# Clamps on GpSimd as a minimum and then a maximum in one instruction, and a semaphore for each down product, in a fused recurrent block

## The chip, the cores and the metric

The kernel runs on one core of a Trainium2 chip. The metric is the device time of one execution in microseconds. The kernel before took 123.34 us (median of three runs, 123.24 to 123.43). The profile is of one execution of its own; in it the first and the last recorded instruction are 121.0 us apart.

Engines: PE is TensorE (PEld its weight loads), DVE is VectorE, ACT is ScalarE, POOL is GpSimd, SP is the engine that issues most DMAs. Each engine takes its instructions strictly in the order in which the program lists them, and waits between engines are semaphores that are counted up.

## The reference

The input x has the shape (8, 512, 128): eight sequences of 512 steps with 128 channels, in float32. Cut to what matters:

```
xn   = layernorm(x)
kin, vin, rin = xn * m + shifted(xn) * (1 - m)        # one m for each of the three
k, v, r = kin @ Wk, vin @ Wv, sigmoid(rin @ Wr)
mx_t  = max(mx_{t-1} + td, k_t)                       # running maximum
den_t = exp(mx + td - mx_t) * den + exp(k - mx_t)     # and the same for the numerator
s    = (r * numerator / denominator) @ Wo
f    = relu(xn @ W1 + b1) @ W2 + b2                   # 128 -> 512 -> 128
g    = silu(layernorm(xn + f) * gamma + beta)
out  = x + s * g
```

## The kernel before

The work is tiled by sequence: b = 0 to 7, each with tiles of 128 channels (partitions) by 512 steps. For each b some fifty steps are named, and the strings in PROGRAM give, engine by engine, the order in which each engine does them; the steps of two or three sequences are interleaved, and most tiles have two buffers, so that b waits for b - 2. BANKS gives each of the eight PSUM banks the list of the results that it holds one after the other; `bank_free` makes a result wait for the last reader of the result before it in its bank (FREED_BY).

The steps that matter here, with the lines of the profile:

- POOL: `norm1:b` (L335, xn, four instructions of 128x128), `d:b` (L365, step_x), `xT_hi:b` and `xT_lo:b` (L349, L356: the transposed input in two fp32r parts), `fix:b` (L374), `gmin:b` (`lower`, L382), `gmax:b` (`upper`, L389), `dv:b` (L396), `keep:b` (L404), `nm` (L326, for groups of sequences).
- `gap:b` (DVE, L729) is k minus the running maximum before it. `gmin:b` is min(gap, td) and `gmax:b` is max(gap, td), td being a column of one value for each partition. ACT makes exp of each: `e_new:b` (L496, from gap_min) and `e_keep:b` (L512, from gap_max).
- DVE then scans `den:b` (L736), ACT takes its logarithm (`ln_den`, L500), DVE makes `rel` (L744), ACT `th_g` and `th_a` (L525, L504), POOL `keep`, DVE scans `dev` (L751), then `adev`, `wkv`, `gated` (L759, L767, L775).
- PE: `T:b` transposes xn (L566), `up0` to `up3` (L601 to L603, three matmuls each in fp32r), `k`, `v`, `r` (L581), `z0` to `z3` (L632, the four down products that add up in one bank), `var` (L618), `s` (L611), `back` (L643). An fp32 product of 512 columns stands in the profile as two matmuls.
- ACT `hid0` to `hid3` (L468) are the relu, `sq` (L477) the square of z + b2, `ln_var`, `rstd2`; DVE `zn` (L784), ACT `silu` (L536), DVE `prod` (L792) and `res` (L801).

The order of POOL between the first clamp and the third sequence is `xT_lo:1 gmax:0 nm:2 gmin:0 norm1:2 gmin:1 gmax:1 dv:0 d:2 xT_hi:2 xT_lo:2`, and later `d:4 fix:4 gmin:3 gmax:3 xT_lo:4 norm1:5`.

Of the four down products of a sequence only the last in PE's order counts a semaphore up, `done["z"]`; `sq:b` waits for it, and `hid` of b waits for that of b - 2.

## Time and profile before

| | |
|---|---|
| median of three runs | 123.34 us |
| lowest, highest | 123.24, 123.43 us |
| the profiled execution | 122.89 us |
| its span, first to last instruction | 121.0 us |
| PE busy | 105.6 us (87%) |
| DVE busy | 96.4 us (80%) |
| ACT busy | 95.0 us (79%) |
| POOL busy | 79.8 us (66%) |
| mean granted TensorE clock | 0.972 of full speed |

The span is shorter than the time by 1.9 us, which lie around it. Busy time counts an instruction from its start to its end. On PE, and to a lesser degree on the others, an instruction starts before the one ahead of it has ended, so that the distance from start to start is shorter than a duration: the pace of two instructions is read from their starts.

### The profile page before, as it was taken

What the parts mean: (1) busy time and instruction counts of PE and PEld (TensorE: products, weight loads), DVE (VectorE), ACT (ScalarE), POOL (GpSimd) and SP (SyncE); (2) the same over time, 40 slices, a digit from 0 to 9 for tenths busy, and PEclk for the clock granted to TensorE, in tenths of its full rate; (3) what the DMA queues carried; (4) which work ended last, traced back from release to release, by engine and by line L of the source; (5) the groups of instructions that cost most, each with busy time, mean ns of one, the idle gap of its engine ahead of it and who ended that gap; (6) DMA issues with size and microseconds to landing.
All of it is one profiled execution on the core that took longest, in us unless ns stands there. A gap on an engine that the chain in (4) does not pass through costs nothing. (4 is left out here: it accounts for less than half of the span.)

```text
span 121.0 us, 1604 instructions
## 1 busy us (share of the span) xinstructions
PE 105.6 (87%) x336; PEld 56.7 (47%) x336; DVE 96.4 (80%) x199; ACT 95.0 (79%) x155; POOL 79.8 (66%) x104
## 2 busy tenths in 40 slices
PE   5996997864999989997599999999979789999770
PEld 5961353613455535642456464465433435544340
DVE  1769897369969599998746789995999396989991
ACT  2361759298969979995769999996999599999960
POOL 2069999986356899269999988946746980380000
PEclk9999999997699999999859999999999999999999
DMA  4999000000000000000000230000000002022035
GB/s 112 270 312 250 12 3 0 5 0 0 0 3 3 0 0 0 0 0 0 0 0 0 87 93 1 0 0 0 0 3 0 3 0 86 1 87 87 5 105 155
DMA packets 9449, 5.09 MB, mean 42 GB/s; under 512 B 480, under 2 KB 9184, under 8 KB 9440
## 3 DMA queue, kind: packets, MB, share of 16 engines
q1 hardware_dynamic: 8880, 4.59, 13.4%
q10 hardware_dynamic: 560, 0.40, 1.3%
q8 instruction: 3, 0.05, 0.2%
q14 instruction: 6, 0.05, 0.1%
HBM read 2.89 MB, written 2.10 MB: 41 GB/s over the span
## 5 line engine op out<-in xcount | busy, mean ns | idle before, releaser
L632 PE MATMUL bank<-hid,w_c 128*128 128x512 f32 x64 | 31.4, 594 | 0.0
L581 PE MATMUL bank<-mixed,w_in 128*128 128x512 f32 x48 | 25.4, 624 | 1.7 <-DVE prod L792 0.6
L468 ACT ACTIVATE hid<-bank,vec 128x512 f32<-128x512 f32 x32 | 21.4, 681 | 2.3 <-PE bank L603 1.9
L601 PE MATMUL bank<-xT_hi,w_hi 128*128 128x512 f32 x28 | 16.5, 588 | 5.3 <-POOL xT_lo L356 5.3
L712 DVE SCALAR_TENSOR_TENSOR mixed<-step_x,vec,bank 128x511 f32<-128x511 f32 x24 | 17.5, 736 | 1.1 <-POOL step_x L365 1.1
L632 PEld LDWEIGHTS bank<-hid,w_c 128*128 128x128 f32 x64 | 12.2, 194 | 10.9 <-issue 9.7
L736 DVE TENSOR_TENSOR_SCAN den<-e_keep,bank 128x512 f32<-128x512 f32 x8 | 9.7, 1216 | 8.2 <-ACT e_keep L512 3.9
L389 POOL TENSOR_SCALAR gap_max<-gap,td 128x512 f32<-128x512 f32 x8 | 12.5, 1561 | 3.8 <-DVE gap L729 3.8
L581 PEld LDWEIGHTS bank<-mixed,w_in 128*128 128x128 f32 x48 | 8.4, 194 | 11.9 <-issue 8.8
L382 POOL TENSOR_SCALAR gap_min<-gap,td 128x512 f32<-128x512 f32 x8 | 12.5, 1561 | 1.9 <-DVE gap L729 1.9
L365 POOL TENSOR_TENSOR step_x<-xT 128x512 f32<-128x512 f32 x8 | 9.0, 1127 | 6.4 <-ACT xT L460 6.3
L396 POOL TENSOR_TENSOR dv<-v_sb 128x512 f32<-128x512 f32 x8 | 9.6, 1205 | 4.8 <-ACT v_sb L519 4.8
L601 PEld LDWEIGHTS bank<-xT_hi,w_hi 128*128 128x128 f32 x28 | 5.5, 197 | 14.8 <-issue 9.5
L335 POOL TENSOR_SCALAR xn<-x_sb,neg_mean,rstd 128x128 f32<-128x128 f32 x28 | 12.1, 446 | 0.0
L751 DVE TENSOR_TENSOR_SCAN dev<-keep,dv 128x512 f32<-128x512 f32 x8 | 9.8, 1224 | 2.3 <-POOL dv L396 1.5
L602 PE MATMUL bank<-xT_hi,w_lo 128*128 128x512 f32 x28 | 11.6, 413 | 0.0
L603 PE MATMUL bank<-xT_lo,w_hi 128*128 128x512 f32 x28 | 11.5, 411 | 0.0
L721 DVE TENSOR_TENSOR_SCAN mx<-td,bank 128x512 f32<-128x512 f32 x8 | 9.7, 1210 | 0.8 <-PE bank L581 0.6
L418 ACT ACT_TABLE_LOAD x6 | 7.7, 1283 | 2.3 <-issue 2.2
L611 PE MATMUL bank<-gated,wo_half 128*128 128x512 f32 (+1 forms) x18 | 8.5, 553 | 0.9 <-DVE gated L775 0.9
L618 PE MATMUL bank<-sq,averager 128*128 128x512 f32 (+1 forms) x18 | 9.1, 601 | 0.1
L512 ACT ACTIVATE e_keep<-gap_max,td 128x512 f32<-128x512 f32 x8 | 5.8, 720 | 4.2 <-POOL gap_max L389 4.2
(70 smaller groups left out, 204.1 us busy)
## 6 DMA issues: line engine op xcount, KB each, us to landing
x_sb<-x SPq DMA_DIRECT2D x7, 256.0 KB, 6.3
block_out<-res SPq DMA_DIRECT2D x7, 256.0 KB, 2.3
w_in<-squares SPq DMA_DIRECT2D x1, 256.0 KB, 3.1
w_in<-w ACTq DMA_DIRECT2D x1, 256.0 KB, 5.6
w_in<-w SPq DMA_DIRECT2D x1, 256.0 KB, 5.9
block_out<-res SPq DMA_DIRECT2D x2, 128.0 KB, 1.9
x_sb<-x ACTq DMA_DIRECT2D x1, 128.0 KB, 2.5
x_sb<-x SPq DMA_DIRECT2D x1, 128.0 KB, 2.2
```

What stands on the lines that cost most here:

```text
L335: pool.tensor_scalar(xn[n][:, j, :], x_tile(b, j), neg_mean1[:, i:i + 1], rstd1[:, i:i + 1], ALU.add, ALU.mult).then_inc(done["norm1"], 1)
L382: pool.tensor_scalar(gap_min[n][:, :], gap[n][:, :], td[:, :], None, ALU.min).then_inc(done["gmin"], 1)
L389: pool.tensor_scalar(gap_max[n][:, :], gap[n][:, :], td[:, :], None, ALU.max).then_inc(done["gmax"], 1)
L468: act.activation(hid[b % 2][:, f, :], ps(f"up{f}", b)[:, :], ACT.Relu, bias=vec[:, B1_COLUMN + f:B1_COLUMN + f + 1]).then_inc(done[f"hid{f ...
L581: pe.matmul(ps(name, b)[:, :], w_in[:, which, :], mixed[b % 2][:, which, :], start=True, stop=True).then_inc(done[name], 1)
L601: pe.matmul(dst, hi, xT_hi[n][:, :], start=True, stop=False)
L602: pe.matmul(dst, lo, xT_hi[n][:, :], start=False, stop=False)
L603: pe.matmul(dst, hi, xT_lo[n][:, :], start=False, stop=True).then_inc(done[f"up{f}"], 1)
L632: ins = pe.matmul(ps("z", b)[:, :], w2_c[:, f, :], hid[b % 2][:, f, :], start=False, stop=last, skip_group_check=True)
L712: dve.scalar_tensor_tensor(mixed[n][:, which, 1:], step_x[n][:, 1:], vec[:, which:which + 1], ps("z", b)[:, 0:T - 1], ALU.mult, ALU.add).t ...
L721: dve.tensor_tensor_scan(mx[n][:, 1:], td[:, 0:1].to_broadcast([P, T]), ps("k", b)[:, :], MX_START, ALU.add, ALU.max).then_inc(done["mx"], 1)
L751: dve.tensor_tensor_scan(dev[n][:, :], keep[n][:, 0:T], dv[n][:, :], 0.0, ALU.mult, ALU.add).then_inc(done["dev"], 1)
```

## The change

Two things are edited and the schedule strings are changed with them. First, `lower` and `upper` get a second operation each: min(gap, td) is followed by a maximum with the most negative float32, and max(gap, td) is preceded by a minimum with the largest float32, so that both are one instruction with a minimum and then a maximum; the values are what they were. Second, each down product counts up a semaphore of its own, `hid{f}:b` waits for product f of b - 2 alone, and `sq:b` waits for the last of the four in PE's order. On PE `z3:0` moves ahead of `z2:0`, and `up1:7` ahead of `z0:6`; on DVE `zn:5` ahead of `inr:7`; on POOL `nm:4` ahead of `xT_hi:3`. Several results move to another PSUM bank. ACT's order and the DMAs stay.

```diff
--- before.py
+++ after.py
...
 MX_START = -1e38
+FP32_MAX = 3.4028234e38
 WARM_UP = 11
...
     "pe": """
-        T:0 up3:0 b2m up2:0 k:0 T:1 up0:0 up1:0 v:0 k:1 up1:1 up0:1 up2:1 z0:0 z1:0 T:2 up3:1 z2:0 z0:1
-        z1:1 z3:0 up3:2 r:0 z3:1 z2:1 k:2 var:0 up2:2 up0:2 v:1 up1:2 z2:2 T:3 z0:2 var:1 s:0 z1:2 r:1
+        T:0 up3:0 b2m up2:0 k:0 T:1 up0:0 up1:0 v:0 k:1 up1:1 up0:1 up2:1 z0:0 z1:0 T:2 up3:1 z3:0 z2:0
+        z0:1 z1:1 up3:2 r:0 z3:1 z2:1 k:2 var:0 up2:2 up0:2 v:1 up1:2 z2:2 T:3 z0:2 var:1 s:0 z1:2 r:1
         v:2 z3:2 up3:3 up2:3 up0:3 r:2 T:4 k:3 up1:3 z0:3 z2:3 var:2 z1:3 k:4 z3:3 up3:4 up0:4 var:3
...
         up2:5 var:4 up1:6 up2:6 up0:5 v:5 T:7 k:6 z0:5 s:3 z2:5 up0:6 z1:5 z3:5 r:5 up3:6 z2:6 k:7 var:5
-        z1:6 up3:7 z0:6 up1:7 z3:6 up0:7 back:2 var:6 v:6 s:4 up2:7 back:3 v:7 z0:7 back:4 z1:7 z2:7 r:6
+        z1:6 up3:7 up1:7 z0:6 z3:6 up0:7 back:2 var:6 v:6 s:4 up2:7 back:3 v:7 z0:7 back:4 z1:7 z2:7 r:6
         r:7 z3:7 s:5 var.a:7 var.b:7 back:5 s:6 s.a:7 back:6 s.b:7 back.a:7 back.b:7
...
         dev:3 adev:3 wkv:3 dev:4 adev:4 wkv:4 gated:3 prod:2 gated:4 mx:5 gap:5 inr:5 ink:6 inv:6 zn:4
-        den:5 mx:6 rel:5 inr:6 prod:3 ink:7 dev:5 adev:5 gap:6 wkv:5 gated:5 mx:7 gap:7 den:6 inr:7 zn:5
+        den:5 mx:6 rel:5 inr:6 prod:3 ink:7 dev:5 adev:5 gap:6 wkv:5 gated:5 mx:7 gap:7 den:6 zn:5 inr:7
         inv:7 res:2 den:7 prod:4 rel:6 zn:6 res:3 rel:7 dev:6 adev:6 res:4 wkv:6 dev:7 gated:6 prod:5
...
         d:0 w1_lo nm:1 fix:0 norm1:1 w2_c d:1 xT_hi:1 fix:1 xT_lo:1 gmax:0 nm:2 gmin:0 norm1:2 gmin:1
-        gmax:1 dv:0 d:2 xT_hi:2 xT_lo:2 keep:0 fix:2 norm1:3 keep:1 gmax:2 gmin:2 dv:1 d:3 xT_hi:3 nm:4
+        gmax:1 dv:0 d:2 xT_hi:2 xT_lo:2 keep:0 fix:2 norm1:3 keep:1 gmax:2 gmin:2 dv:1 d:3 nm:4 xT_hi:3
         fix:3 xT_lo:3 norm1:4 dv:2 keep:2 xT_hi:4 d:4 fix:4 gmin:3 gmax:3 xT_lo:4 norm1:5 norm1:6 gmax:4
...
 z:0 s:0 up0:3 up1:3 k:4 k:5 k:7 s:6 back:6
-up3:0 up0:0 v:0 up2:2 up1:2 var:1 r:1 z:4 s:3 r:5 up3:7 up0:7 s:4 v:7
-b2m z:1 up2:3 k:3 s:2 up1:6 up0:6 up3:6 var:5 up1:7 var:6 up2:7 r:6 var.a:7
-up2:0 k:1 v:2 var:3 z:5 back:2 back:3 back:4 var.b:7
-k:0 var:0 v:1 up3:3 r:2 up0:4 up2:4 up1:5 z:6
+up3:0 up0:0 v:0 up2:2 up1:2 var:1 r:1 k:3 s:2 up1:6 up0:6 up3:6 var:5 up1:7 back:2 back:3 back:4 var.b:7
+b2m z:1 up3:3 r:2 up0:4 up2:4 up3:5 r:4 up2:6 z:7
+up2:0 k:1 v:2 var:3 z:5 up0:7 s:4 v:7
+k:0 var:0 v:1 up2:3 z:4 s:3 r:5 up3:7 var:6 up2:7 r:6 var.a:7
 up1:0 up1:1 r:0 up0:2 z:3 v:4 up2:5 v:5 v:6 s:5 back:5 s.b:7 back.b:7
-up0:1 up3:1 up3:2 k:2 var:2 up3:4 up1:4 back:0 back:1 up3:5 r:4 up2:6 z:7
+up0:1 up3:1 up3:2 k:2 var:2 up3:4 up1:4 back:0 back:1 up1:5 z:6
 up2:1 z:2 s:1 v:3 r:3 var:4 up0:5 k:6 r:7 s.a:7 back.a:7
...
                  + [f"up{f}" for f in range(NF)] + [f"hid{f}" for f in range(NF)]
-                 + ["z", "sq", "var", "ln_var", "rstd2", "zn", "silu", "prod", "back", "res"])
+                 + [f"z{f}" for f in range(NF)] + ["sq", "var", "ln_var", "rstd2", "zn", "silu", "prod", "back", "res"])
         done = {n: sem(f"done_{n}") for n in STEPS}
...
                     after(eng, step, previous[2], previous[1])
+
+        def chunks_of(b):
+
+            return [name for name, _, i in tokens("pe") if name in CHUNKS and i == b]
...
                 after(pool, "e_new", b - 2)
-                pool.tensor_scalar(gap_min[n][:, :], gap[n][:, :], td[:, :], None, ALU.min).then_inc(done["gmin"], 1)
+                pool.tensor_scalar(gap_min[n][:, :], gap[n][:, :], td[:, :], -FP32_MAX,
+                                   ALU.min, ALU.max).then_inc(done["gmin"], 1)
...
                 after(pool, "e_keep", b - 2)
-                pool.tensor_scalar(gap_max[n][:, :], gap[n][:, :], td[:, :], None, ALU.max).then_inc(done["gmax"], 1)
+                pool.tensor_scalar(gap_max[n][:, :], gap[n][:, :], FP32_MAX, td[:, :],
+                                   ALU.min, ALU.max).then_inc(done["gmax"], 1)
...
                     after(act, f"up{f}", b)
-                    after(act, "z", b - 2)
+                    after(act, f"z{f}", b - 2)
                     act.activation(hid[b % 2][:, f, :], ps(f"up{f}", b)[:, :], ACT.Relu,
...
                 once(act, b, "cols", 4)
-                after(act, "z", b)
+                after(act, chunks_of(b)[-1], b)
                 after(act, "var", b - 2)
...
                 pe.wait_ge(got["vec"], 16)
+                bank_free(pe, "b2m", None)
                 pe.wait_ge(prep["consts"], 2)
...
                     once(pe, b, "w2", 1)
-                    order = [name for name, _, i in tokens("pe") if name in CHUNKS and i == b]
-                    if order[0] == f"z{f}":
+                    if chunks_of(b)[0] == f"z{f}":
...
                     after(pe, f"hid{f}", b)
-                    last = order[-1] == f"z{f}"
-                    ins = pe.matmul(ps("z", b)[:, :], w2_c[:, f, :], hid[b % 2][:, f, :], start=False, stop=last,
-                                    skip_group_check=True)
-                    if last:
-                        ins.then_inc(done["z"], 1)
+                    pe.matmul(ps("z", b)[:, :], w2_c[:, f, :], hid[b % 2][:, f, :], start=False,
+                              stop=chunks_of(b)[-1] == f"z{f}", skip_group_check=True).then_inc(done[f"z{f}"], 1)
                 return step
...
```

## Rows read from the trace of the kernel before

**Rows 1.** page: busy us, share of the span and count, by engine

```profile
PE 105.6 (87%) x336; PEld 56.7 (47%) x336; DVE 96.4 (80%) x199; ACT 95.0 (79%) x155; POOL 79.8 (66%) x104
```

**Rows 2.** POOL by line and form; behind the bar busy us, mean ns

```profile
L389 POOL TENSOR_SCALAR gap_max<-gap,td 128x512 f32<-128x512 f32 x8 | 12.5, 1561 | 3.8 <-DVE gap L729 3.8
L382 POOL TENSOR_SCALAR gap_min<-gap,td 128x512 f32<-128x512 f32 x8 | 12.5, 1561 | 1.9 <-DVE gap L729 1.9
L335 POOL TENSOR_SCALAR xn<-x_sb,neg_mean,rstd 128x128 f32<-128x128 f32 x28 | 12.1, 446 | 0.0
...
L404 POOL TENSOR_SCALAR keep<-th_g 128x512 f32<-128x512 f32 x8 | 5.0, 620 | 3.5 <-ACT th_g L525 3.5
...
L374 POOL TENSOR_SCALAR mixed<-vec,step_x 128x3 f32<-128x3 f32 x8 | 2.6, 331 | 3.4 <-PE bank L581 3.2
...
L326 POOL TENSOR_SCALAR neg_mean<-mv 128x16 f32<-128x16 f32 x1 | 0.3, 266 | 0.0
...
L326 POOL TENSOR_SCALAR neg_mean<-mv 128x4 f32<-128x4 f32 x1 | 0.2, 239 | 0.0
```

**Rows 3.** timeline of POOL: start us, duration us, line, operation [idle before]

```profile
16.32 1.56 POOL L389 TENSOR_SCALAR gap_max<-gap,td 128x512 f32<-128x512 f32 x1
...
22.87 1.56 POOL L389 TENSOR_SCALAR gap_max<-gap,td 128x512 f32<-128x512 f32 x1
```

**Rows 4.** timeline of ACT, the exponentials behind the first clamps and the last

```profile
22.93 0.69 ACT L496 ACTIVATE bank<-gap_min,neg_td 128x512 f32<-128x512 f32 x1 [1.89 <-POOL gap_min L382]
24.47 0.72 ACT L512 ACTIVATE e_keep<-gap_max,td 128x512 f32<-128x512 f32 x1 [0.85 <-POOL gap_max L389]
...
96.21 0.69 ACT L496 ACTIVATE bank<-gap_min,neg_td 128x512 f32<-128x512 f32 x1 [1.47 <-POOL gap_min L382]
```

**Rows 5.** timeline of PE: start us, duration us, line [idle before <-releaser]

```profile
28.84 0.76 PE L601 MATMUL bank<-xT_hi,w_hi 128*128 128x512 f32 x1 [2.57 <-POOL xT_lo L356]
...
46.11 0.71 PE L601 MATMUL bank<-xT_hi,w_hi 128*128 128x512 f32 x1
...
58.72 0.47 PE L601 MATMUL bank<-xT_hi,w_hi 128*128 128x512 f32 x1 [1.89 <-POOL xT_lo L356]
...
71.30 1.88 PE L632 MATMUL bank<-hid,w_c 128*128 128x512 f32 x4
...
74.31 2.88 PE L581 MATMUL bank<-mixed,w_in 128*128 128x512 f32 x6
...
88.73 1.10 PE L581 MATMUL bank<-mixed,w_in 128*128 128x512 f32 x2 [0.61 <-DVE prod L792]
...
94.78 0.47 PE L601 MATMUL bank<-xT_hi,w_hi 128*128 128x512 f32 x1 [0.67 <-POOL xT_lo L356]
```

**Rows 6.** stretches: engines' busy us, then granted clock, DMA share, GB/s

```profile
16.00:28.80 12.80, 9.11 (x29) 4.76 (x28) 8.88 (x19) 8.53 (x16) 12.29 (x14) 1.00 0.01 1
28.80:32.00 3.20, 3.16 (x6) 1.87 (x7) 3.03 (x7) 2.58 (x5) 0.62 (x1) 0.51 0.00 0
34.00:56.00 22.00, 21.59 (x66) 11.40 (x66) 19.64 (x40) 19.82 (x33) 16.18 (x21) 1.00 0.00 1
59.50:62.80 3.30, 3.30 (x7) 1.94 (x6) 2.44 (x4) 2.01 (x4) 3.30 (x7) 0.51 0.00 0
```

**Rows 7.** timeline of POOL: step_x twice, a clamp, xT_lo

```profile
41.85 1.77 POOL L365 TENSOR_TENSOR step_x<-xT 128x512 f32<-128x512 f32 x1 [0.32 <-ACT xT L460]
...
52.82 1.04 POOL L365 TENSOR_TENSOR step_x<-xT 128x512 f32<-128x512 f32 x1
...
54.24 1.56 POOL L382 TENSOR_SCALAR gap_min<-gap,td 128x512 f32<-128x512 f32 x1
...
57.30 1.26 POOL L356 TENSOR_TENSOR xT_lo<-xT,xT_hi 128x512 fp32r<-128x512 f32 x1
```

**Rows 8.** timeline of DVE: a scan, and a scaling step

```profile
41.57 1.23 DVE L751 TENSOR_TENSOR_SCAN dev<-keep,dv 128x512 f32<-128x512 f32 x1 [1.48 <-POOL dv L396]
...
45.80 0.74 DVE L784 SCALAR_TENSOR_TENSOR zn<-bank,cb,rstd 128x512 f32<-128x512 f32 x1
```

## The prediction

> **What bounds the kernel now.** I read the page's busy times first. PE is busy 87% of the span, DVE 80%, ACT 79%, POOL 66% [rows 1]. Nobody is full, so no busy sum gives the time: it is set by a loop of hand-overs that goes from engine to engine, and the question is which waits end last. The chain of waits is of little use here, because it covers the last 6 us alone. So I went on to POOL's groups by line and form, where the sixteen clamps stand out at 1561 ns each [rows 2], then to the timelines of POOL, ACT, PE and DVE side by side from 16 us on, where the first clamp starts, and to the stretches.
>
> What is to be seen there: from 16.0 to 28.8 us POOL is busy 12.29 of 12.80 us, while PE has 9.11, DVE 8.88 and ACT 8.53 [rows 6]. In this stretch POOL is the bound. ACT waits 1.89 us for gmin:1 and 0.85 us for gmax:1 [rows 4], then transposed input, its two parts and up3:2 follow, and PE stands still for 2.57 us before up3:2 [rows 5]. Behind that idle time the granted clock is 0.51, that is 1.2 GHz instead of 2.4, for 3.2 us. The same happens once more: PE waits 1.89 us for xT_lo:4 [rows 5], and from 59.5 to 62.8 the clock is 0.51 again [rows 6]. Between these, from 34 to 56 us, PE is busy 21.59 of 22.00 us at full clock [rows 6] and is itself the bound. Later PE waits 0.61 us for prod:3 and 0.67 us for xT_lo:7 [rows 5], and ACT 1.47 us for gmin:6 [rows 4].
>
> **What a clamp will cost.** The trace has no clamp with two operations, so I bound it. Of the form of today, one operation and none behind it, there is also neg_mean: 239 ns with 4 columns and 266 ns with 16, which is 27/12 = 2.3 ns per column; the clamp itself has (1561 - 239)/508 = 2.6 ns per column [rows 2]. The instructions with two real operations are another kind: keep (multiply, add, both immediates) takes 620 ns for 512 columns, so (620 - 239)/508 = 0.75 ns per column. xn (add, multiply, both from columns of values) takes 446 ns for 128 [rows 2]. So what is slow looks like the missing second operation, not the minimum. That is read from neg_mean, a multiplication that is as slow per column as the clamps, though over so few columns a fixed cost could look the same. The column operand td costs a little: mixed, with one such operand and 3 columns, has 331 ns, against 239. I take 620 ns plus about 70 for td, 0.69 us. The near bound above is xn stretched out: 331 + (446 - 331)/125 x 509 = 799 ns; below it is keep's 0.62. The far bound above is 1.56 us, nothing gained. Beyond it, if each of the two operations costs what one costs now, 239 + 2 x 2.6 x 512 = 2.9 us. I take 0.69 because keep and xn both are tensor_scalar with two operations, the form that the clamps get. What speaks against it is that both have arithmetic and no minimum. A clamp then saves 1.56 - 0.69 = 0.87 us, sixteen of them 14 us of POOL; only what stands on the path counts.
>
> A rule speaks against this change. The Trainium skill, GPSIMD Engine Reference, section 3.1, has a cost per element that depends on the number of ALU operations in the body: with two or fewer the port is the limit, at 1.03 cycles, with more it rises. By that rule a second operation never makes a body faster, and the sum below would be nought. The rows do not fit it as they stand: the body with one operation takes 3.5 times as long per column as keep's with two [rows 2].
>
> **The sum, stage by stage.** First, 16.3 to 28.8 us. gmax:0 starts at 16.32 [rows 3]; nm, gmin:0, the four xn, gmin:1 and gmax:1 follow without a gap, and e_keep:1, which waits for gmax:1, starts at 24.47 [rows 4]. Four clamps lie in a row: 4 x 0.87 = 3.5 us. The next wait in the list is T:2 for hid2:1, which moves by 1.2 us with the earlier e_keep:0; PE then has some 4.6 us of transposes, up and z products to do and arrives at up3:2 about when xT_lo:2 is there. So e_keep:1, xT:2, xT_lo:2 and up3:2 all come 3.5 us earlier, and the 2.57 us of idle PE nearly vanish. Without that idle time I expect no fall of the clock: 3.2 us of work at half clock become 1.6, another 1.6 us less. ACT, busy for only 2.58 us of the 3.20, can follow for the most part [rows 6].
>
> Second, 34 to 56 us: PE is the bound, gmax:2 and gmin:2 are ahead of dv:1, for which DVE waits 1.48 us [rows 8]. Two clamps save 1.74 us, the wait is gone, and PE gains the little that it stands idle in this stretch, 22.00 - 21.59 = 0.4 us [rows 6]. The rest is hidden behind PE.
>
> Third, 54 to 64 us: gmin:3 starts at 54.24, gmax:3 follows, and xT_lo:4 starts at 57.30 only behind both [rows 7]; it releases PE's 1.89 us. Two clamps give 1.74 us. Again the clock should hold: 3.3 us at 0.51 become 1.65 [rows 6]. Together 3.4 us. ACT is busy for only 2.01 of those 3.30 us [rows 6], and waits for both clamps ahead of them, so it can follow.
>
> Fourth, from 64 us to the end: PE's 0.61 us for prod:3 goes, because den:5 is behind gmax:5. Then gmax:6 is ahead of xT_lo:7 and of gmin:6, for which PE waits 0.67 and ACT 1.47 us [rows 4, 5]. The next limit is sq:6, which waits for the last product of z:6 and so for PE; I take 1.3 of the 1.47. Together 1.9 us. Behind that ACT has no idle time until its last silu, and what is gained arrives at the end.
>
> That makes 3.5 + 1.6 + 0.4 + 3.4 + 1.9 = 10.8 us. In five places I found the next wait less than 0.2 us away (hid2:1 ahead of T:2, xT_lo ahead of up3:2 and of up3:4, zn:1 ahead of up3:3, gap:7 ahead of gmin:7). I take off 0.2 us for each, 1.0 us, which leaves 9.8. The profiled execution of 122.89 us (121.0 of span, 1.9 around it) would become 113.1; the median was 0.45 us above it, so **113.5 us**.
>
> **The other edits.** Products that each count up a semaphore: the projections do this on every second matmul, the down products only at the end. Six of the former take 2.88 us, four of the latter 1.88, 0.48 and 0.47 us each [rows 5]. So an increment costs nothing that can be seen; bounds are 0 and 24 x 0.01 = 0.24 us. The Trainium skill, TensorE: Matmul & The Clock Gate, section "The cost: per-tile semaphore tail", has 26.3 ns for each increment of tiles that end together, and recommends one on the last; 24 more would be 0.63 us by it. The two rows show none of that for full-size products.
>
> The finer wait of hid on z gives nothing, as no row has ACT waiting for a down product. The wait of sq is for the same product as before. The banks are where an edit can cost. up3:3 now waits for zn:1 (before: wkv:1). zn:1 runs from 45.80 to 46.54 [rows 8], up3:3 started at 46.11 [rows 5]: 0.43 us of PE, with the rest of PE's queue behind it, k:3 and T:4 first, and ACT's relu steps wait for that. With fast clamps DVE has its 1.48 us back by then and zn:1 is in time; I take 0, and 0.43 if the cover is gone. up0:7 now waits for zn:5, which is moved ahead of inr:7 for it, 0 to 0.3 us likewise. nm:4 ahead of xT_hi:3 moves 0.27 us within POOL and nothing ahead of xT_lo:3, so 0. up1:7 ahead of z0:6 brings hid1:7 forward and lets z0:6 wait, 0.
>
> **The rivals.** (a) The clock falls all the same, or the thin places are thicker than read: a wait of an engine takes the place of POOL's, PE still idles before up3:2 and up3:4, and the two slow stretches stay, 3.3 us. 113.5 + 3.3 gives 116.8, range 116.5 to 119.5. For it: 79 to 80% busy ACT and DVE leave them little room, and DVE's scans slow POOL (step_x took 1.77 us beside the dev scan, 1.04 without [rows 7, 8]), which short clamps meet at new places. Against it: in four stretches alone ACT has 4.27 + 0.62 + 2.18 + 1.29 = 8.4 us of idle time, and DVE 3.92 + 0.17 + 2.36 + 0.86 = 7.3 [rows 6], so that there is room for what these stretches are to give back, 3.5 + 1.6 + 0.4 + 1.65.
>
> (b) The second operation changes nothing, clamps stay at 1.56 us (this is what the rule of section 3.1 comes to). Then the schedule alone decides: zn:1 costs 0.43 us, zn:5 0 to 0.3, and up1:7, brought forward, may give back 0.1 or 0.2: 123.34 + 0.3 = 123.6, from 123.2 to 124.3.
>
> (c) Slower than before: a minimum and a maximum are compare steps that the core works off one after the other. It decides from any clamp over about 1.56 us. At 1.95 us (0.75 ns per column added, keep's rate) ten clamps on the path, four in the first stage and two in each of three more, cost 10 x 0.39 = 3.9 us, so 127.6 with the bank's 0.4; at 2.9 us it is 137.
>
> **How the numbers follow.** Chances: forecast 0.64, with 110.8 to 116.5 as its own range (clamps of 0.62 and no thin place at the low end; clamps of 0.8 to 0.9 and thin places of double size at the other); (a) 0.19; (b) 0.10; (c) 0.07. The forecast's and (a)'s ranges hold together 0.81, so the range is 110.8 to 119.5 and leaves (b) and (c) out. A measurement of this kernel can tell about 0.2%, 0.25 us, from no change. Faster: 0.64 + 0.19 + 0.01 of (b) = 0.84. Same: 0.04 of (b). Slower: 0.05 of (b) and 0.07 of (c), 0.12.
>
> **What would show it.** Clamp rows of L382 and L389 near 690 ns, POOL busy some 14 us less. PE's waits for xT_lo (2.57, 1.89 and 0.67 us [rows 5]) nearly gone. The granted clock at full speed in all slices after the start, and no stretch at 0.51. ACT's waits for gap_min and gap_max (1.89, 0.85 and 1.47 us among them [rows 4]) gone but for a few tenths. If the clamps are fast and the time stays above 117, the steps about the clock and the thin places are wrong; if they are at 1.56 or above, the step about the missing second operation is.

## The result

The changed kernel takes 112.18 us (median of four runs, 111.57 to 112.55); the kernel before had 123.37 us in the same comparison. The ratio is 0.909, with a 95% interval from 0.905 to 0.913: 11.2 us less, where 9.8 were forecast. The profiled execution has 112.55 us and a span of 110.7; that is 10.3 us less than the one shown of before.

The page of the changed kernel, with the lines that answer to [rows 1] (busy us and share of the span), and the granted clock in 40 slices:

```profile
PE 101.9 (92%) x336; PEld 56.7 (51%) x336; DVE 96.0 (87%) x199; ACT 94.3 (85%) x155; POOL 66.0 (60%) x104
...
PEclk9999999999999999999999999999999999999998
```

DVE and ACT have about the same work in less time (within 0.7 us), PE 3.7 us less, mostly because its products no longer run at half clock, and POOL 13.8 us less. In this execution the clock stays at full speed up to the last slice; the four executions have mean clocks of 0.991 to 0.996.

POOL's groups by line and form, as in [rows 2] (busy us, mean ns behind the bar):

```profile
L395 POOL TENSOR_SCALAR gap_max<-gap,td 128x512 f32<-128x512 f32 x8 | 5.5, 690 | 3.6 <-DVE gap L733 3.5
L387 POOL TENSOR_SCALAR gap_min<-gap,td 128x512 f32<-128x512 f32 x8 | 5.5, 687 | 2.7 <-DVE gap L733 2.5
...
L411 POOL TENSOR_SCALAR keep<-th_g 128x512 f32<-128x512 f32 x8 | 5.0, 623 | 3.4 <-ACT th_g L532 3.3
```

The clamps went from 1561 to 690 and 687 ns, which is the 0.69 us of the forecast; keep is as before (620 and 623 ns).

The timeline of PE in the changed kernel, the first product of up3:2, up3:3 and up3:4, then r:5 and up3:7 (start us, us, line [idle before <-releaser]):

```profile
26.76 0.47 PE L609 MATMUL bank<-xT_hi,w_hi 128*128 128x512 f32 x1 [0.57 <-POOL xT_lo L361]
...
42.39 0.47 PE L609 MATMUL bank<-xT_hi,w_hi 128*128 128x512 f32 x1 [0.17 <-POOL xT_lo L361]
...
52.92 0.47 PE L609 MATMUL bank<-xT_hi,w_hi 128*128 128x512 f32 x1 [0.19 <-POOL xT_lo L361]
...
80.48 1.02 PE L589 MATMUL bank<-mixed,w_in 128*128 128x512 f32 x2
...
85.20 0.67 PE L609 MATMUL bank<-xT_hi,w_hi 128*128 128x512 f32 x1
```

The waits for xT_lo are 0.57, 0.17 and 0.19 us where they were 2.57, none and 1.89, the one for prod:3 (80.48) is gone and so is the one before up3:7 (85.20). ACT's waits for both clamps, 8.5 us in ten places before, leave 0.72 us at gmax:0 and 0.38 at gmin:1. Three of the places in the timeline of ACT (no bracket means no wait):

```profile
21.72 0.69 ACT L503 ACTIVATE bank<-gap_min,neg_td 128x512 f32<-128x512 f32 x1 [0.38 <-POOL gap_min L387]
22.39 0.72 ACT L519 ACTIVATE e_keep<-gap_max,td 128x512 f32<-128x512 f32 x1
...
85.75 0.69 ACT L503 ACTIVATE bank<-gap_min,neg_td 128x512 f32<-128x512 f32 x1
```

A stretch of each stage, as in [rows 6] (engines' busy us, then granted clock, DMA share, GB/s):

```profile
25.00:28.00 3.00, 2.43 (x8) 1.09 (x7) 2.98 (x8) 2.97 (x5) 2.15 (x3) 1.00 0.00 0
30.00:50.00 20.00, 19.83 (x63) 10.72 (x62) 18.96 (x44) 19.50 (x33) 12.69 (x21) 1.00 0.00 1
...
56.00:80.00 24.00, 24.00 (x82) 13.21 (x81) 22.26 (x31) 23.69 (x38) 18.58 (x25) 1.00 0.08 23
```

From 56 to 80 us PE is busy all the time, ACT 23.69 of 24.00 us: there PE is the bound, with ACT next to it. From 25 to 28 us it isn't PE (2.43 of 3.00 us busy) but DVE and ACT that are full, with 2.98 and 2.97.

To compare kernels whose start differs by up to a us, I use five marks that every trace has: the start of gmax:0 on POOL, of up3:2, up3:4 and r:5 on PE, and of the last transposes back. The four distances between them are below, worked out from the starts in each trace (distance 1 is from the first mark to the second, and so on):

```
kernel                      starts of the marks, us                  1      2      3      4
before              16.32   28.84   58.72   88.73  117.31    12.52  29.88  30.01  28.58
changed             17.49   26.76   52.92   80.48  106.96     9.27  26.16  27.56  26.48
e1 clamps only      17.45   26.70   52.83   80.39  106.86     9.25  26.13  27.56  26.47
e2 changed again    16.73   25.98   52.10   79.66  106.15     9.25  26.12  27.56  26.49
e3 old clamps       16.50   29.02   58.86   88.88  117.48    12.52  29.84  30.02  28.60
e4 semaphores only  17.26   29.81   59.77   89.85  118.44    12.55  29.96  30.08  28.59
e6 short in 0, 1    16.87   26.11   54.83   84.84  113.42     9.24  28.72  30.01  28.58
e7 short in 2 to 4  16.54   29.06   55.19   83.65  112.23    12.52  26.13  28.46  28.58
e8 filled, long     17.03   31.13   60.61   89.64  118.22    14.10  29.48  29.03  28.58
e9 short in 4       16.74   29.25   59.20   90.14  118.73    12.51  29.95  30.94  28.59
e10 short in 5 to 7 16.60   29.13   58.76   87.87  114.35    12.53  29.63  29.11  26.48
e11 reversed order  17.45   31.94   62.48   94.33  124.22    14.49  30.54  31.85  29.89
e12 filled, first   16.71   29.23   57.92   87.93  116.51    12.52  28.69  30.01  28.58
```

The gain of the changed kernel is 3.25 + 3.72 + 2.45 + 2.10 = 11.5 us from the first clamp on; in the execution shown it starts 1.17 us later, which leaves 10.35.

### The profile page after: what moved, and what is told of

Its sections match the earlier page's. It is cut to its first block and busy times, and to the rows that moved or that the text cites. A ratio compares the mean times of both kernels' runs of the same rounds, so it can differ in the third digit from the quotient of the medians.

```text
span 110.7 us, 1604 instructions
## 1 busy us (share of the span) xinstructions
PE 101.9 (92%) x336; PEld 56.7 (51%) x336; DVE 96.0 (87%) x199; ACT 94.3 (85%) x155; POOL 66.0 (60%) x104
## 5 line engine op out<-in xcount | busy, mean ns | idle before, releaser
L589 PE MATMUL bank<-mixed,w_in 128*128 128x512 f32 x48 | 24.1, 599 | 0.8 <-POOL mixed L379 0.7
L638 PEld LDWEIGHTS bank<-hid,w_c 128*128 128x128 f32 x64 | 11.9, 190 | 10.8 <-issue 9.3
L609 PE MATMUL bank<-xT_hi,w_hi 128*128 128x512 f32 x28 | 15.5, 552 | 1.1 <-POOL xT_lo L361 1.1
L370 POOL TENSOR_TENSOR step_x<-xT 128x512 f32<-128x512 f32 x8 | 8.3, 1037 | 8.5 <-ACT xT L467 8.4
L611 PE MATMUL bank<-xT_lo,w_hi 128*128 128x512 f32 x28 | 11.0, 395 | 0.0
L610 PE MATMUL bank<-xT_hi,w_lo 128*128 128x512 f32 x28 | 11.0, 394 | 0.0
L467 ACT ACTIVATE xT<-bank 128x512 f32<-128x512 f32 x8 | 4.8, 598 | 6.1 <-PE bank L574 6.1
L361 POOL TENSOR_TENSOR xT_lo<-xT,xT_hi 128x512 fp32r<-128x512 f32 x7 | 8.9, 1268 | 0.1
L626 PE MATMUL bank<-sq,averager 128*128 128x512 f32 (+1 forms) x18 | 8.2, 549 | 0.1
```

The costliest lines, as they stand in the source:

```text
L589: pe.matmul(ps(name, b)[:, :], w_in[:, which, :], mixed[b % 2][:, which, :], start=True, stop=True).then_inc(done[name], 1)
L609: pe.matmul(dst, hi, xT_hi[n][:, :], start=True, stop=False)
L610: pe.matmul(dst, lo, xT_hi[n][:, :], start=False, stop=False)
L611: pe.matmul(dst, hi, xT_lo[n][:, :], start=False, stop=True).then_inc(done[f"up{f}"], 1)
L638: pe.matmul(ps("z", b)[:, :], w2_c[:, f, :], hid[b % 2][:, f, :], start=False, stop=chunks_of(b)[-1] == f"z{f}", skip_group_check=True).th ...
```

## The experiments

**Which edit it was.** Four kernels. The first has only this edit of the kernel before:

```diff
-                pool.tensor_scalar(gap_min[n][:, :], gap[n][:, :], td[:, :], None, ALU.min).then_inc(done["gmin"], 1)
+                pool.tensor_scalar(gap_min[n][:, :], gap[n][:, :], td[:, :], -FP32_MAX,
+                                   ALU.min, ALU.max).then_inc(done["gmin"], 1)
...
-                pool.tensor_scalar(gap_max[n][:, :], gap[n][:, :], td[:, :], None, ALU.max).then_inc(done["gmax"], 1)
+                pool.tensor_scalar(gap_max[n][:, :], gap[n][:, :], FP32_MAX, td[:, :],
+                                   ALU.min, ALU.max).then_inc(done["gmax"], 1)
```

> The kernel before with one edit: both clamps as a minimum and then a maximum. Order, banks and semaphores stay as before. My theory is that the whole gain comes from the clamps, 1.56 to 0.69 us each: the time is that of the changed kernel, 112.2, or up to 0.5 us more or less by the order and the banks. The rival is that the new order and banks are needed to carry the gain to the end: then 114 to 116 us.

> The changed kernel once more, as the measure for its neighbours: 112.2 us, clamps of 0.69 us.

Measured: 112.03 us for the clamps alone (ratio 0.911, 0.907 to 0.914) and 111.76 for the changed kernel again (0.909, 0.906 to 0.911). The distances of the two are equal within 0.02 us. Order, banks and semaphores aren't needed to carry the gain, so the rival of 114 to 116 us is out.

The third is the changed kernel with that edit taken back, the fourth the kernel before with the semaphores alone:

```diff
-                    after(act, "z", b - 2)
+                    after(act, f"z{f}", b - 2)
...
-                    if last:
-                        ins.then_inc(done["z"], 1)
+                              stop=order[-1] == f"z{f}", skip_group_check=True).then_inc(done[f"z{f}"], 1)
```

> The changed kernel with the clamps of before (one operation each), new order, banks and semaphores kept. My theory: clamps at 1.56 us again, and the bank of up3:3 (it waits for zn:1) costs 0.43 us, so 123.6, from 123.2 to 124.3. Rival: order and banks are worth something by themselves, then under 122.5. Second rival: they fit short clamps alone and cost over 1 us with long ones, 124.5 or more.

> The kernel before with one edit: each down product counts up its own semaphore, hid waits for product f of b - 2. Theory: no change, 123.1 to 123.6, as no wait of ACT for a down product is in the trace. Rival, at 26 ns for each of 24 more increments: 124.0.

Measured: 123.28 us (ratio 1.001, 0.999 to 1.004) and 123.68 us (1.004, 1.001 to 1.008). New order, banks and semaphores together are worth nothing by themselves. The first time lies in the expected range, but not for the reason given with it; the second is just above its own (123.6). The stall of up3:3 for zn:1 is there, but it is not paid for. This is PE's timeline in the kernel before, where the projection ahead of up3:3 starts, and then in e3:

```profile
44.64 1.10 PE L581 MATMUL bank<-mixed,w_in 128*128 128x512 f32 x2 [0.41 <-DVE adev L759]
```

```profile
44.73 1.10 PE L587 MATMUL bank<-mixed,w_in 128*128 128x512 f32 x2 [0.40 <-DVE adev L761]
...
46.70 0.50 PE L607 MATMUL bank<-xT_hi,w_hi 128*128 128x512 f32 x1
...
58.86 0.47 PE L607 MATMUL bank<-xT_hi,w_hi 128*128 128x512 f32 x1 [1.80 <-POOL xT_lo L361]
```
And this is DVE's timeline in the same kernel, the step that gives zn:1:

```profile
45.90 0.74 DVE L786 SCALAR_TENSOR_TENSOR zn<-bank,cb,rstd 128x512 f32<-128x512 f32 x1
```

zn:1 ends at 46.64, and up3:3 starts at 46.70, 1.97 us behind the projection at 44.73; before, that was 46.11 - 44.64 = 1.47 [rows 5]. Yet up3:4 is where it was. Counted from the start of the trace, e3 is 0.18 us behind the kernel before at up3:2, 0.09 at the projection, 0.59 at up3:3, but only 0.24 at the next projection, r:2 (48.90 against 48.66) and 0.14 at up3:4. So most of the 0.5 us is gone before the wait for xT_lo:4, which got only 0.09 us shorter (1.80 in place of 1.89); part of it is in the reading, since in the kernel before up3:3 starts while the product ahead of it still runs, and at its second product the lag is 0.37 (47.03 against 46.66).

For the semaphores the four distances are 0.03, 0.08, 0.07 and 0.01 us longer than before, 0.2 us together. The median, 123.68 against 123.15, says more than that, but it compares unlike executions. Both kernels have some with a mean clock of 0.970 to 0.972 and some with 0.986. Those of 0.970 to 0.972 have a median of 123.13 us in both. Those of 0.986 take 123.67 to 124.00 us in e4, and 123.43 to 123.96 in the kernel before beside the later experiments. In e4 six of ten are of the second kind, in the kernel before, beside it, five of nineteen. The profiled e4 is of that kind, and its first clamp starts at 17.26 us, against 16.32, where no down product has run yet. So what the record gives the semaphores is 0.2 us at most.

**What makes a clamp short.** Twelve instructions of 128x512 behind POOL's last step in the kernel before, each once and each behind the end of the one before it, on one input and into a tile of their own. Their edit:

```diff
+            for s1, s2, op0, op1 in PROBES:
+                column_or = lambda v: td[:, :] if v == "td" else v
+                pool.tensor_scalar(probe_tile[:, :], rel[0][:, :], column_or(s1), column_or(s2), op0,
+                                   *([op1] if op1 is not None else [])).then_inc(done["probe"], 1)
```

> The kernel before, with twelve tensor_scalar instructions of 128x512 more at the end of GpSimd's work, each behind a semaphore, in this order: (min td, none), (mult 0.5, none), (mult td, none), (min 0.5, none), (min td, max constant), (max constant, min td), (min td, mult 1.0), (min td, add 0), (mult 1.0, min td), (mult 1.0, add 0), (mult td, add 0.5), (min td, min td). Their output goes to a tile that nobody reads; the time of the whole says nothing. My theory, the missing second operation makes a body slow: the first four take 1.5 to 1.6 us, mult no less than min, and all eight others 0.60 to 0.80. Rival A, only the order minimum and then maximum has a fast body, and arithmetic pairs have: then (max, min), (min, mult), (min, add), (min, min) take 1.5 us or more. Rival B, min and max are slow alone and mult is fast alone: the two mult probes with none take 0.6 to 0.7.

The timeline of POOL, one row for each probe in that order (start us, us):

```profile
113.96 1.56 POOL L432 TENSOR_SCALAR probe_tile<-rel,td 128x512 f32<-128x512 f32 x1 [3.79 <-DVE adev L785]
115.61 1.50 POOL L432 TENSOR_SCALAR probe_tile<-rel 128x512 f32<-128x512 f32 x1
117.20 1.57 POOL L432 TENSOR_SCALAR probe_tile<-rel,td 128x512 f32<-128x512 f32 x1
118.85 1.49 POOL L432 TENSOR_SCALAR probe_tile<-rel 128x512 f32<-128x512 f32 x1
120.44 0.69 POOL L432 TENSOR_SCALAR probe_tile<-rel,td 128x512 f32<-128x512 f32 x1
121.24 2.00 POOL L432 TENSOR_SCALAR probe_tile<-rel,td 128x512 f32<-128x512 f32 x1
123.33 2.00 POOL L432 TENSOR_SCALAR probe_tile<-rel,td 128x512 f32<-128x512 f32 x1
125.43 2.00 POOL L432 TENSOR_SCALAR probe_tile<-rel,td 128x512 f32<-128x512 f32 x1
127.53 2.00 POOL L432 TENSOR_SCALAR probe_tile<-rel,td 128x512 f32<-128x512 f32 x1
129.62 0.62 POOL L432 TENSOR_SCALAR probe_tile<-rel 128x512 f32<-128x512 f32 x1
130.34 0.69 POOL L432 TENSOR_SCALAR probe_tile<-rel,td 128x512 f32<-128x512 f32 x1
131.13 2.06 POOL L432 TENSOR_SCALAR probe_tile<-rel,td 128x512 f32<-128x512 f32 x1
```

The first four, with one operation, take 1.49 to 1.57 us whether they are a minimum or a multiplication. With two operations there are two kinds: (min, max) 0.69, (mult, add) 0.62 and 0.69 with td; but (max, min), (min, mult), (min, add) and (mult, min) 2.00 and (min, min) 2.06. So my theory was right for one operation and wrong for two: in five of the eight probes with two the instruction gets slower, by 0.4 to 0.5 us, and only certain pairs in a certain order are short, as rival A had it. Whether td stands in the first or the second place doesn't matter: gmin has it first and gmax second, and they take 687 and 690 ns. Of the pairs tried these are minimum before maximum and multiply before add; xn's add and multiply, 446 ns for 128 columns, looks like a third by [rows 2]; it was not probed at 512. Why these and not the others is open: no run shows the code that GpSimd works them off with.

The same on the whole kernel, the clamps of before with their two operations the other way round:

```diff
-                pool.tensor_scalar(gap_min[n][:, :], gap[n][:, :], td[:, :], None, ALU.min).then_inc(done["gmin"], 1)
+                pool.tensor_scalar(gap_min[n][:, :], gap[n][:, :], -FP32_MAX, td[:, :],
+                                   ALU.max, ALU.min).then_inc(done["gmin"], 1)
...
+                pool.tensor_scalar(gap_max[n][:, :], gap[n][:, :], td[:, :], FP32_MAX,
+                                   ALU.max, ALU.min).then_inc(done["gmax"], 1)
```

> The kernel before with both operations in the clamps, but a maximum and then a minimum. The probe of this order took 2.00 us. Theory: clamps of 2.0 us, 0.44 more than before; the short clamps gave some 10 us for 0.87 less each, so about 12 us per us of a clamp: 5 us more than before, 127 to 130. Rival, only the order of the probes made it slow: 112.

Measured: 129.61 us, ratio 1.051 (1.046 to 1.056). POOL's groups by line and form:

```profile
L383 POOL TENSOR_SCALAR gap_min<-gap,td 128x512 f32<-128x512 f32 x8 | 15.9, 1994 | 2.1 <-DVE gap L732 1.9
L391 POOL TENSOR_SCALAR gap_max<-gap,td 128x512 f32<-128x512 f32 x8 | 15.9, 1990 | 3.8 <-DVE gap L732 3.7
```

That is inside the expected 127 to 130 us, and here, too, td's place makes no difference (first or second, 1.99 us). The same values come out, and which of the two operations stands first decides between 9% faster and 5% slower.

**Where the gain is.** The short clamps in some sequences only, on the kernel before; the edit is this, with other numbers in each:

```diff
+                if b in (0, 1):
+                    pool.tensor_scalar(gap_min[n][:, :], gap[n][:, :], td[:, :], -FP32_MAX,
+                                   ALU.min, ALU.max).then_inc(done["gmin"], 1)
+                else:
```

> The kernel before, with two operations only in the clamps of sequences 0 and 1, the other twelve as before. Theory: 3.1 to 3.5 us from the four clamps in a row and 1.6 from the clock that doesn't fall at 28.8 us, so 4.7 to 5.1 less than before, 118.0 to 118.7. Rival (the clock falls all the same, or the work of that stretch waits for others): 119.6 to 120.2. Second rival, the gain is taken back by PE's later waits for GpSimd: over 121.

> The kernel before, with two operations only in the clamps of sequences 2, 3 and 4. Theory: 0.0 to 0.4 us from sequence 2, 1.7 from gmin:3 and gmax:3 ahead of xT_lo:4, 1.6 from the clock at 59.5 us, so 3.3 to 3.8 less than before, 119.3 to 119.9. Rival: without the clock, 121.2 to 121.5.

> The kernel before, with two operations only in the clamps of sequences 5, 6 and 7. From the differences of the earlier traces: 0.9 us up to r:5 on PE and 2.1 us behind it, 3.0 together, 120.2 to 120.7. Rival, my prediction's 1.9: 121.2 to 121.6.

Measured: 119.16 us for sequences 0 and 1 (ratio 0.966, 0.960 to 0.971), 119.73 for 2 to 4 (median of four; the ratio, 0.961, 0.951 to 0.971, is of the two shortest alone) and 120.33 for 5 to 7 (0.976, 0.971 to 0.981). In the distances, e6 has 3.28 us in the first and 1.16 in the second; e7 has 3.75 in the second and 1.55 in the third; e10 has 0.90 in the third and 2.10 in the fourth, as expected of it, and 0.25 in the second, where the fall of the clock was a little shorter. The changed kernel has 3.72 in the second and not 1.16 + 3.75, because e7's execution, too, was one without a fall (below). The four times of e7 are 117.82, 120.28, 119.52 and 119.94 us, at mean granted clocks of 1.000, 0.977, 0.985 and 0.986. So its median lies in the expected range, but the traced execution has none of the two falls, where the expectation had the first one stay; against the traced one the others are 1.7 to 2.5 us longer, more than the 1.2 us that a fall is found to cost below, and that difference is open.

e6 missed its range, 118.0 to 118.7, by 0.5 us: the first fall gave 1.16 us in the second distance and not 1.6. The traces show where the rest went. With the fall (the kernel before) PE is through with the product ahead of v:2 and starts to wait for adev:1 15.39 us behind up3:2; without it (e12, below) that is 13.78 us, 1.61 less. But the wait is then 0.84 us and not 0.41, and takes 0.43 back.

**What the clock cost.** The kernel before, slow clamps kept, with small products (128 columns, identity by identity) on PE ahead of its waits; they go into the bank that up3 overwrites next:

```diff
+FILL = {(3, 2): 16, (3, 4): 14}
...
+                    for _ in range(FILL.get((f, b), 0)):
+                        pe.matmul(dst[:, 0:P], ident[:, :], ident[:, :], start=True, stop=True)
                     after_split(pe, "xT_hi", b)
```

> The kernel before with slow clamps; PE gets 16 small products (128 columns, identity by identity) into the bank of up3:2 ahead of its wait for xT_lo:2, and 14 ahead of up3:4, so that it is not idle there. The result is not touched. Theory: the clock stays at full speed behind both, the stretches of 3.2 and 3.3 us at 0.51 take half, and the time is 3.2 us less at most, 120.1 to 121.3 (ACT and DVE may hold up a part). Rival, the half clock cost nothing at the end because others paced these stretches: 122.8 to 123.6.

Measured: 123.75 us, ratio 1.003 (1.000 to 1.006), which looks like the rival. But the trace shows that the experiment spoils itself. The 16 products are 32 matmuls and take 3.84 us, more than the wait (timeline of PE in e8):

```profile
27.54 3.84 PE L600 MATMUL bank<-ident 128*128 128x128 f32 x32 [0.56 <-ACT hid L469]
31.13 0.48 PE L604 MATMUL bank<-xT_hi,w_hi 128*128 128x512 f32 x1
```

up3:2 comes 14.10 us behind the first clamp, 1.6 more than before; the next two distances are 0.4 and 1.0 us shorter, which pays that back but for 0.2 us. The second filling, too, ends behind the arrival of xT_lo:4, so neither says what a fall costs. So it was done once more with half the products and in the first place alone, `FILL = {(3, 2): 8}`:

> The kernel before with slow clamps; PE gets 8 small products into the bank of up3:2 ahead of its wait for xT_lo:2, which end before xT_lo:2 is there (16 of them ran 1.6 us over). Theory: the first fall of the clock is gone and gives 1.2 us, 121.9 to 122.4. Rival: it costs nothing at the end, 123.0 to 123.6.

PE's timeline in it, and the two waits that got longer or are new, for adev:1 and for zn:3:

```profile
27.21 2.05 PE L600 MATMUL bank<-ident 128*128 128x128 f32 x16 [0.56 <-ACT hid L469]
29.23 0.47 PE L604 MATMUL bank<-xT_hi,w_hi 128*128 128x512 f32 x1
...
43.85 1.10 PE L582 MATMUL bank<-mixed,w_in 128*128 128x512 f32 x2 [0.84 <-DVE adev L762]
...
67.05 1.10 PE L582 MATMUL bank<-mixed,w_in 128*128 128x512 f32 x2 [1.38 <-DVE zn L787]
```

Now they end as xT_lo:2 arrives, up3:2 is in place (12.52), the clock is at full speed in the whole trace, and the time is 122.16 us (median of nine), ratio 0.991 (0.989 to 0.994): 1.2 us, as expected. The second distance gives 29.88 - 28.69 = 1.19. So the first fall costs 1.2 us at the end, though PE itself gains the 1.6 of its half work: the wait for adev:1 takes 0.4 back. In the same trace the clock doesn't fall at up3:4 either, and there the third distance is 30.01, as before. e6 says the same: full clock, and 30.01. Taken alone, the second fall costs nothing at the end. The last line above says why: at full clock PE is ready for v:4 7.75 us behind up3:4 and not 9.24, 1.49 earlier, but then waits 1.38 us for zn:3. On DVE zn:3 stands behind den:4, and den:4 waits for e_new:4, that is for gmin:4 on POOL. At half clock there is no such wait.

What it was hidden behind, e9 was to show:

> The kernel before, with two operations only in gmax:4 and gmin:4. Both stand behind xT_lo:4 and eight xn on GpSimd, so they can't shorten PE's wait for xT_lo:4, and a clock that falls there falls as before. Theory A, the third stretch is paced by GpSimd's row gmin:3, gmax:3, xT_lo:4, xn, gmax:4, gmin:4: 1.5 us less, 121.5 to 122.1. Theory B, the one of my prediction, the half clock of PE paces it: no change, 123.1 to 123.6.

Measured: 124.33, 124.28, 124.08 and 122.10 us, with mean granted clocks of 0.971, 0.971, 0.969 and 0.982; that is not one population, and so no ratio is given. Three of the four lie above the range of either theory. The fourth lies at the edge of theory A's; its mean clock says that it has less of the falls than the others, but it has no trace. In the profiled execution, the first of these, the third distance is 30.94 us, 0.9 more than before. POOL's timeline in e9, the clamps of sequence 4 and xn behind them:

```profile
62.58 0.69 POOL L395 TENSOR_SCALAR gap_max<-gap,td 128x512 f32<-128x512 f32 x1
63.24 0.68 POOL L384 TENSOR_SCALAR gap_min<-gap,td 128x512 f32<-128x512 f32 x1
65.53 1.74 POOL L336 TENSOR_SCALAR xn<-x_sb,neg_mean,rstd 128x128 f32<-128x128 f32 x4 [1.60 <-PE bank L575]
```
ACT's timeline in e9, hid1:4 and the first exponential:

```profile
63.86 0.69 ACT L477 ACTIVATE hid<-bank,vec 128x512 f32<-128x512 f32 x1 [0.59 <-PE bank L612]
64.45 0.71 ACT L521 ACTIVATE e_keep<-gap_max,td 128x512 f32<-128x512 f32 x1
```

ACT's timeline in e6, where the clock stays up and the clamps of sequence 4 are long:

```profile
59.69 0.73 ACT L521 ACTIVATE e_keep<-gap_max,td 128x512 f32<-128x512 f32 x1 [0.82 <-POOL gap_max L398]
61.23 0.69 ACT L505 ACTIVATE bank<-gap_min,neg_td 128x512 f32<-128x512 f32 x1 [0.81 <-POOL gap_min L387]
```

In e9 the clamps are short and the clock falls: hid1:4 waits 0.59 us for PE, and POOL, instead of pacing, waits 1.60 us for PE's transposes. In e6 the clock is up and the clamps are long: ACT waits 0.82 and 0.81 us for them.

The 0.9 us are another matter. Up to T:6 PE is where it was, 14.27 us behind up3:4 and 14.30 before; then it waits 0.64 us for adev:3. The scan dev:3 on DVE ahead of adev:3 takes 1.99 us. From the timelines of POOL, DVE and PE in e9, POOL's dv:4, the scan and PE's wait:

```profile
71.72 1.03 POOL L405 TENSOR_TENSOR dv<-v_sb 128x512 f32<-128x512 f32 x1
71.84 1.99 DVE L760 TENSOR_TENSOR_SCAN dev<-keep,dv 128x512 f32<-128x512 f32 x1 [0.38 <-issue]
74.70 1.10 PE L620 MATMUL bank<-gated,wo_half 128*128 128x512 f32 x2 [0.64 <-DVE adev L768]
```

The scan and dv:4 in the kernel before:

```profile
71.26 1.22 DVE L751 TENSOR_TENSOR_SCAN dev<-keep,dv 128x512 f32<-128x512 f32 x1 [0.27 <-issue]
71.61 1.71 POOL L396 TENSOR_TENSOR dv<-v_sb 128x512 f32<-128x512 f32 x1 [0.43 <-ACT v_sb L519]
```

The two disturb each other, and in these rows it is the one that starts later that gets long: dv:4 (1.71 us, 1.03 alone) where the scan is 0.35 us ahead, the scan (1.99 us, 1.22 alone) where dv:4 is 0.12 us ahead. Here DVE's scan is on the path and dv:4 is not. With the next scan, 1.38 us for 1.22, that is 0.77 + 0.16 = 0.93 us, all that e9 has lost. In the changed kernel the scan is ahead by only 0.18 us (63.92 and 64.10).

So two paths of about equal length lead through this stretch, PE at half clock and POOL's row gmin:3, gmax:3, xT_lo:4, xn, gmax:4, gmin:4. Faster clamps alone give PE nothing up to T:6 (e9), full clock alone gives nothing (e6, e12); in e7 and in the changed kernel both are gone, and the third distance is 1.55 us shorter in e7. No run takes both away and leaves gmin:3 and gmax:3 long; that these two clamps have no part in the 1.55 us is read from the traces, as they end ahead of up3:4.

## Why the prediction was right

The forecast of 113.5 us was 1.3 above the measured time, which lies inside the range of 110.8 to 119.5. The path was right: POOL's clamps ahead of PE's waits, and the clock behind them. Missing in the sum are the 1.0 us taken off for the thin places, which cost nothing, and 1.1 us in the fourth stage; 0.4 us too much in the first and third go the other way. Step by step:

- A clamp of 0.69 us: measured 0.687 and 0.690. The number is right, the reason only half. "What is slow looks like the missing second operation" holds against (mult, none); but that two operations are short was inferred from keep and xn, which happen to be short pairs. With the maximum put first the same inference would have given the same 0.69, and 2.00 is measured. What I put against it, that both rows are arithmetic and have no minimum, was the right doubt and deserved more than rival (b) and (c) together with 0.17.
- First stage: 4 x 0.87 = 3.5 forecast, 3.25 measured. POOL's row starts to wait for others: from the start of gmax:0 to that of dv:0 it took 8.08 us and now takes 4.83, with gaps of 0.1 us ahead of nm:2 and of gmin:0 that weren't there. PE still waits 0.57 us for xT_lo:2.
- Its clock and the second stage: 1.6 and 0.4 forecast, 2.0 together, and 2.0 measured, but otherwise divided. PE gains 1.61 us from the clock, as forecast, but as long as the clamps of sequence 2 are long the wait for adev:1 behind dv:1 grows from 0.41 to 0.84 us and leaves 1.2 (e12, e6). The short clamps then take away 0.85 us of wait and not 0.41. The sum counted both in full, which is right for the changed kernel and too much for either alone.
- Third stage, the two clamps ahead of xT_lo:4: 1.74 forecast; the second distance is 28.72 - 26.16 = 2.56 shorter than e6's, less 0.85 for the wait just named, 1.7.
- Its clock: 1.65 forecast, and by itself 0. PE gains 1.49 us from it in e12 and loses 1.38 in the wait for zn:3. The 1.55 us need the clamps of sequence 4 as well, which I had left out of the sum. The size was right, the condition was missing: I had looked at whether ACT can follow, and not at what DVE's den:4 and zn:3 wait for. That the changed kernel fulfils it was not foreseen, and so is luck.
- Fourth stage: 1.9 forecast, 0.90 + 2.10 = 3.0 measured (e10). Here is the largest miss in size. I capped ACT's 1.47 us at 1.3 for sq:6; but PE, for which sq:6 waits, has its own idle time of 0.67 us before up3:7 and 0.55 before back:2 gone, beside the 0.61 for prod:3 and the wait of den:5 behind gmax:5.
- The thin places, 1.0 us taken off, cost nothing that can be seen: zn:1 ahead of up3:3 was in time, as were hid2:1 and gap:7. Without that allowance the sum is 10.8, and the distances give 11.5.
- The other edits at nothing: right (e1 equals the changed kernel; e3 is at 1.001). The price of 0.43 us for up3:3 without its cover was about right as a stall (0.5 us in the starts, 0.28 at its second product) and wrong as a cost: at up3:4 nothing of it is left.
- Increments: the traces show at most 0.2 us in 24 increments, below the upper bound of the forecast (0.24). The Trainium skill, TensorE: Matmul & The Clock Gate, "The cost: per-tile semaphore tail", would give 0.63 us; e4's distances don't bear it out for products of 512 columns.
- The rule that spoke against the change, in the Trainium skill, GPSIMD Engine Reference, section 3.1, has one pace for bodies of up to two operations and a slower one for more. By it a second operation changes nothing; (min, none) at 1.56, (min, max) at 0.69 and (min, mult) at 2.00 us contradict it both ways.
- Rival (a) did not come up in the changed kernel, whose executions have mean clocks of 0.991 and above. It did in e7, whose clamps of the first stage are long: 119.5 to 120.3 us with a lower mean clock and 117.82 without.
- Rival (c) did not come true for the pair that was chosen, but its price is real for the other order, e11. At 2.0 us it costs 6.3 us; by my count of ten clamps it would have been 4.4.

## What to carry to other kernels

On GpSimd, a tensor_scalar of this kind (128x512, float32) is to be written as one of the pairs that are short here, minimum then maximum or multiply then add, with a constant that changes nothing as the other part, and its duration is to be read from the trace, since the same operations in another order take three times as long. A wait is worth what is left when the next wait is reached; where two paths of equal length run side by side (here PE at half clock and a row of POOL), removing either alone shows nothing, and both must be taken before the gain is seen. A step that gets faster can come to run beside another at a new place: look at the durations of the other engines, too, when a kernel gets slower than it should (the scan of e9). When the clock falls behind an idle stretch, fill that stretch with work that ends in time, and compare the distances between marks, not only the time.

## What the runs showed of the hardware that I had not expected

The pace of a pair of operations on GpSimd: 0.62 to 0.69 us for (min, max) and (mult, add) and 2.00 to 2.06 for five other pairs at the same 128x512, with one operation between them at 1.49 to 1.57.

An idle time of 2.57 us before up3:2 doesn't always bring the clock down. e7's profiled execution has the same 2.57 us and stays at full clock. The granted clock in 40 slices, from the page of e7:

```profile
PEclk9999999999999999999999999999999999999999
```
The wait in e7, from PE's timeline:

```profile
29.06 0.47 PE L610 MATMUL bank<-xT_hi,w_hi 128*128 128x512 f32 x1 [2.57 <-POOL xT_lo L357]
```

In e4, with the same wait before up3:2 and 1.92 us before up3:4, the page has one fall and not two:

```profile
PEclk9999999999589999999999999999999999999999
```

And that one comes later than in the kernel before, where the first 3.2 us from up3:2 on have 0.51 [rows 6]. The same stretch in e4 and the next (engines' busy us, then granted clock, DMA share, GB/s):

```profile
29.80:33.00 3.20, 3.19 (x7) 1.78 (x8) 3.03 (x7) 3.20 (x6) 1.34 (x3) 0.68 0.00 0
33.00:36.20 3.20, 3.20 (x8) 1.23 (x7) 1.95 (x8) 2.04 (x3) 1.92 (x5) 0.78 0.04 8
```

The clock is 0.68 in the first stretch and 0.78 in the second. So at the same wait the fall comes at once, later or not at all from one execution to the next. e3 and e4, whose third distances are 30.02 and 30.08 with no fall at up3:4, are two more executions in which the missing second fall doesn't shorten the time.

In the executions of the kernel before, those with a mean clock of 0.986 were not shorter than those with 0.970 to 0.972: beside the last four experiments 123.43 to 123.92 us against 122.99 to 123.22. The profiled e4, with 0.986, has its first clamp 0.94 us later than the profiled execution of before, with 0.972, and from there on it is no shorter.

Up to 1.2 us of difference lie ahead of the first clamp, 0.7 of it in PE's warm-up, with a granted clock of 1.00 in the record in both. The 22 small matmuls at the start take 4.35 us in the kernel before, from its timeline:

```profile
1.51 4.35 PE L550 MATMUL bank<-ident 128*128 128x128 f32 x22 [1.51 <-POOL ident L308]
```
In the changed kernel the same 22 take 5.06 us:

```profile
1.51 5.06 PE L557 MATMUL bank<-ident 128*128 128x128 f32 x22 [1.51 <-POOL ident L313]
```

What decides when PE gets fast there isn't settled; it was not tried.
